# One block for turning back, gate, mix, norm and convolution; earlier turns and an early first load in the routed stages

## The reference

```
y   = gated sum of eo (expert by sequence type), s0, s1 (two shared ones)
        gate_in = concat(eo[:, 0], s0[:, 0], s1[:, 0])      # first token of each sequence
        w = softmax(relu(gate_in @ g1) @ g2)                # 3 weights a sequence
        y = eo * w[:, 0] + s0 * w[:, 1] + s1 * w[:, 2]
h   = layernorm(y); h = causal depthwise convolution of 3 taps, by channel
y   = y + attention(h)
h   = layernorm(y); e = argmax(h @ router)                  # 4 experts
y   = y + (silu(h @ Wgate[e]) * (h @ Wvalue[e])) @ Wdown[e]
out = x + y
```

## Time and profile before

| | us |
|---|---|
| median of 3 runs | 2322.33 |
| lowest, highest | 2319.68, 2323.14 |
| profiled execution, its own time | 2319.53 |
| its span, first to last instruction | 2317.7 |

### The profile page before, as it was taken

How to read it: one execution, slowest core, us unless ns; L and a number is a source line. 1 busy time by engine, 2 the same in 40 slices (tenths; PEclk the granted TensorE clock), 3 DMA queues, 4 the chain that set the end, 5 groups by cost and what they waited for, 6 DMA issues and landing times. The chain is left out here.

```text
span 2317.7 us, 32452 instructions
## 1 busy us (share of the span) xinstructions
PE 2104.6 (91%) x11748; PEld 1784.8 (77%) x11748; DVE 1213.9 (52%) x1983; ACT 906.6 (39%) x1780; POOL 763.5 (33%) x845
## 2 busy tenths in 40 slices
PE   7999999999999999999986887998996469968998
PEld 6888888888888888888875676786996158847997
DVE  3333444334443444344448993433783966657886
ACT  4232323333242323333222994122553224445554
POOL 3030302102030302103012894020783475407884
PEclk9999999999999999999997898999997688978999
DMA  4010000101010000200003003200561030036661
GB/s 156 1 55 1 36 18 0 55 0 54 0 54 0 36 18 0 79 0 0 1 2 81 25 34 119 73 10 0 182 211 62 18 82 35 34 127 220 205 200 56
DMA packets 85644, 135.73 MB, mean 59 GB/s; under 512 B 9726, under 2 KB 64000, under 8 KB 85568
## 3 DMA queue, kind: packets, MB, share of 16 engines
q1 hardware_dynamic: 78512, 118.72, 15.9%
q0 software_dynamic: 4928, 12.86, 1.6%
q10 hardware_dynamic: 2128, 3.15, 0.4%
HBM read 106.91 MB, written 12.06 MB: 51 GB/s over the span
## 5 line engine op out<-in xcount | busy, mean ns | idle before, releaser
L581 DVE TENSOR_TENSOR cond_h<-cond_silu,ps 128x512 f32<-128x512 f32 x288 | 197.9, 687 | 697.7 <-ACT cond_silu L492 694.3
L492 ACT ACTIVATE cond_silu<-ps 128x512 f32<-128x512 f32 x288 | 172.3, 598 | 772.6 <-PE ps L411 772.6
L411 PE MATMUL ps<-a_x_hi,cond_w_hi 128*128 128x512 f32 x1152 | 449.8, 390 | 2.0 <-DVE a_x_lo L261 2.0
L411 PE MATMUL ps<-a_x_lo,cond_w_hi 128*128 128x512 f32 x1152 | 449.2, 390 | 0.0
L411 PE MATMUL ps<-a_x_hi,cond_w_lo 128*128 128x512 f32 x1152 | 449.1, 390 | 0.0
L380 POOL TENSOR_TENSOR cond_w_lo<-cond_stage_up,cond_w_hi 128x256 fp32r<-128x256 f32 x144 | 108.6, 773 | 833.2 <-ACT cond_w_hi L473 833.2
L411 PEld LDWEIGHTS ps<-a_x_hi,cond_w_hi 128*128 128x128 f32 x1152 | 217.0, 188 | 47.3 <-DVE a_x_lo L261 2.4
L411 PEld LDWEIGHTS ps<-a_x_hi,cond_w_lo 128*128 128x128 f32 x1152 | 216.9, 188 | 45.2
L411 PEld LDWEIGHTS ps<-a_x_lo,cond_w_hi 128*128 128x128 f32 x1152 | 217.0, 188 | 44.9
L427 PE MATMUL ps<-cond_h_hi,cond_d_hi 128*128 128x512 f32 x576 | 224.4, 390 | 3.4 <-DVE cond_h_lo L549 3.4
L427 PE MATMUL ps<-cond_h_hi,cond_d_lo 128*128 128x512 f32 x576 | 224.1, 389 | 0.0
(11 more groups left out here) (358 smaller groups left out, 4380.8 us busy)
## 6 DMA issues: line engine op xcount, KB each, us to landing
moe_stage_up<-in_L_ffn_expert_wv SPq DMA_DIRECT2D x22, 1024.0 KB, 10.0
typed_stage_up<-in_L_cond_wi SPq DMA_DIRECT2D x11, 1024.0 KB, 4.9
typed_stage_dn<-in_L_cond_wo SPq DMA_DIRECT2D x11, 1024.0 KB
moe_stage_dn<-in_L_ffn_expert_proj SPq DMA_DIRECT2D x11, 1024.0 KB, 5.6
cond_stage_up<-in_L_cond_Wg SPq DMA_DIRECT2D x7, 1024.0 KB, 4.9
cond_stage_up<-in_L_cond_Wu SPq DMA_DIRECT2D x7, 1024.0 KB, 6.9
cond_stage_dn<-in_L_cond_Wd SPq DMA_DIRECT2D x7, 1024.0 KB, 5.2
hyp_v_now<-hyp_v_blk SPq DMA_DIRECT2D x16, 272.0 KB, 2.3
```

Of the source, the lines that this page charges most:

```text
L411: ins = pe.matmul(up_ps[st % 2][j], w[:, j, k, fs], x[:, k, tok], start=(i == 0), stop=(i == 3 * KC - 1))
L492: act.activation(silu[:, st % 2], up_ps[st % 2][0], ACT.Silu).then_inc(act_done, 1)
L581: dve.tensor_tensor(h[:, st % 2], silu[:, st % 2], up_ps[st % 2][1], ALU.mult).then_inc(up_free, 1)
```

## The change

The three blocks `turn_back`, `mix_gate` and `layer_norm` for ln1 become one, `join`:

- SP waits for the scatters inside the block, loads the first rows of the 32 sequences, [32, 256], and then the four tiles. The gate's matmuls on `s0` and `s1` start at once; those on the typed rows use the 32 turned first rows.
- The second gate weight is spread over 128 columns by ACT (`wide`), so that the logits come out on every partition, [128, 3, 32], and DVE's softmax gives the weights there.
- ACT scales the typed rows by sequence while it takes them from PSUM (8 instructions a tile). DVE adds `s0` and `s1` with 16 scalar_tensor_tensor of [128, 2, 64] a tile, each with the weight of one sequence as its scalar. POOL scales nothing.
- ACT's second affine step writes the last tap's product directly (`wt`, `bt`), so the convolution is two scalar_tensor_tensor per channel block. The inverse root stays in PSUM.
- Gate, norm, tap and attention weights are loaded by SP at the end of the typed stage (`LoadLate`), into the right side of SBUF.

In the routed stages the next rows are turned at f = 1, rounded at 2, split at 3, and ACT copies the residual half (`keep_rows`) at f = 5. In moe, expert 0 gets at least one slot (`known_first`), so slot 0 is always expert 0's, and its weights are loaded during ln2. For typed, the up weights of slot 1 are now loaded after the lists are found.

The diff, cut to its core:

```diff
+class JoinWeights:
-class GateWeights:
-def mix_gate(nc, m, gate, eo, s0, s1, w):
+def join(nc, m, eo_rows, sent, sumT, s0, s1, gate, rope):
...
+            def _(sp):
+                wait_sent(sp, sent)
+                sp.dma_start(first[:], eo_rows.rearrange("(b t) d -> b t d", t=T)[:, 0, :]).then_inc(first_loaded, 16)
+                rows = eo_rows.rearrange("(i p) d -> p i d", p=P)
+                for t in range(TT):
+                    i = slice(t * SUB, (t + 1) * SUB)
+                    sp.dma_start(y[:, i], rows[:, i]).then_inc(row_loaded[t], 16)
...
+                turn(0)
+                turn(1)
+                steps((0, means), (0, lambda t: turn(t + 2) if t + 2 < TT else None), (1, variances))
...
+                    for b in range(BT):
+                        n = t * BT + b
+                        ins = act.activation(sumT[:, :, seq(t, b)], eo_ps[t % 2][:, :, b * T:(b + 1) * T], ACT.Copy, scale=w[:, 0, n:n + 1])
...
+                        act.activation(h[:, t % 2, c, :, PAD:], x, ACT.Identity,
+                                       bias=gate.bcol[:, c:c + 1], scale=gate.wcol[:, c:c + 1]).then_inc(h_done, 1)
+                        act.activation(by_batch(convT[:, c, tile(t)]), x, ACT.Identity,
+                                       bias=bt[:, c:c + 1], scale=wt[:, c:c + 1]).then_inc(tapped, 1)
...
+                scale(0)
+                scale(1)
+                steps((2, affine), (0, lambda t: scale(t + 2) if t + 2 < TT else None), (1, inverse), (0, square))
...
+                    for j, x in ((1, s0), (2, s1)):
+                        for b in range(BT):
+                            n, at = t * BT + b, (slice(None), slice(None), seq(t, b))
+                            ins = dve.scalar_tensor_tensor(sumT[at], x[at], w[:, j, n:n + 1], sumT[at], ALU.mult, ALU.add)
...
+                mix(0)
+                mix(1)
+                steps((0, centre), (2, convolve), (0, lambda t: mix(t + 2) if t + 2 < TT else None), (1, normalize))
...
+        if self.known_first:
+            link(dve.tensor_scalar(self.used[:, 0:1], self.used[:, 0:1], 1.0, None, ALU.max))
...
     def sync(self, sp):
         sp.wait_ge(self.lists.owned, 1)
-        self.slots.load_first(sp, self.lists.found)
+        e = self.slots.expert(sp, 1)
+        self.slots.load_up(sp, e, 1)
+        sp.wait_ge(self.lists.found, 1)
+        self.slots.load_down(sp, e, 1)
...
-                        if f == 4 and not is_last(s):
+                        if f == 1 and not is_last(s):
                             turn(s + 1, nth + q, 1 - q)
...
-                            if f == 5:
+                            if f == 2:
                                 round_x(s + 1, 1 - q)
+                            if f == 5 and carried:
+                                keep_rows(s + 1, 1 - q)
...
-                    if carried:
-                        dve.tensor_copy(keep[:, q], x_row[:, q, :, D:]).then_inc(kept, 1)
...
-                        if f == 6 and not is_last(s):
+                        if f == 3 and not is_last(s):
                             split_x(s + 1, 1 - q)
...
-def turn_back(nc, m, tag, src, dst, early):
...
+                routed_ffn(nc, m, "typed", False, slots, LoadLate(joining, rope))
+            join(nc, m, m.typed_rows, sent, m.sumT, s0, s1, joining, rope)
...
+                           sync_late=lambda sp: slots.load_slot(sp, 0, 0))
```

436 lines of the change are left out of this document (233 added, 203 removed).

## The result

The changed kernel takes 2287.94 us (median of 4 runs, 2287.34 to 2288.22) against 2321.01 for the kernel before in the same comparison (2316.54 to 2323.14): a ratio of 0.9858, interval 0.9844 to 0.9871. The prediction was 2286, with 2272 to 2301 as its range. The profiled execution took 2287.70, its span is 2285.9.

What follows compares the result with a forecast made beforehand. TensorE was taken to bound the typed stage, so gains lay in the join and the last stage's start and waits. 27.1 + 6.3 + 3.0 = 36.4 us off 2319.53 gives 2283.1, plus 2.8 for the median: 2286, range 2272 to 2301.

Steps and rivals of the forecast that it cites:

- The join, behind the weights: Join from gate weights to last convolution: 47.1 us instead of 59.6, a gain of 12.5 us.
- the order of the walk: Join behind the gates: scaling, mixes, centring, normalising and convolutions followed in written order, last convolution ending at 47.1 us.
- The join, ahead of the weights: Join up to the gate weights: first rows fetched ahead of the tiles, gates at about 1779, a gain of 14.6 us.
- The rival in which they come no sooner: Join: first rows arrive no sooner than the tiles, 5 us less gain, 2291; chance 0.05.
- Typed slots, and loads behind them: Typed routed stage: the earlier turn gains 0, and the late weight loads and attention-weight splitting cost nothing.
- The last stage, its start: Start of last stage: slot 0's early expert load and sooner gathered rows bring the first turn 9.1 us earlier, net 6.3.
- The give-back: Last stage, slot 0: a VectorE cast waits for GpSimd's run, a late hidden difference gives 2.6 us back.
- The loop: Last stage's loop: waits for split rows go, half returns as lateness of hidden differences; gain 3.0 us, bounds 0 and 6.3.
- GpSimd's pace: Rival, last stage: GpSimd sets the pace, the stage gains 4 instead of 9.3 us, 2291; chance 0.2.
- The port held for one instruction: Rival, last stage: casts never wait out a GpSimd run, start keeps 9.1 us and loop 6.3, 2280; chance 0.08.
- Dear small pieces: Rival, join: steps 0.35 us apart and TensorE at 1.2 GHz, join gains 20 us, 2293; chance 0.13.
- The slower case: Rival, routed slots: the turn at step 1 waits for its gather; 2336 if landing takes 20 us; chance 0.02.

Runs made afterwards that it cites:

- e6: Changed kernel with 15 extra matmuls, results unused, behind TensorE's last matmul of the typed stage; 2284.49 us, ratio 0.9843 to the kernel before.
- e11: Changed kernel with slot 1's down weights held, three differences on VectorE, tile t+2 turned before tile t's means, 8 extra matmuls behind the typed stage; 2281.33 us.
- e3: Changed kernel with the 32 first rows loaded behind the four tiles; 2287.04 us, ratio 0.9867 to the kernel before.
- e1: Changed kernel with turn, rounding and splitting of the next rows back at steps 4, 5 and 6, kept rows still on ScalarE; 2289.31 us.
- e8: Changed kernel with only slot 1's down weights (1 MB) held until slot 0's gathered rows have landed; 2286.88 us.
- e2: Changed kernel with slot 0's expert loaded only once the owners are known, as before the change; 2291.44 us.
- e7: Changed kernel with the kept rows copied by VectorE again at step 5, the turn staying at step 1; 2289.10 us.
- e10: Changed kernel with three of slot 0's eight weight differences formed by VectorE, slot 1's loads unchanged; 2287.71 us.
- e9: Changed kernel with slot 1's down weights held until slot 0's rows have landed, and three of slot 0's eight differences on VectorE; 2284.16 us.
- e12: The e11 kernel with further extra matmuls in TensorE's waits around attention, results unused; 2278.03 us, ratio 0.9824 to the kernel before.

## Why the prediction came out right, and where its steps were off

**The join, behind the weights: right in length, its reason incomplete.** 47.57 us against 47.1. The price of the fused steps (17.4 us against 18.2), VectorE as the bound and the order of the walk held. But "the 24 larger steps removed cost 29.4" is their price beside GpSimd; alone they are about 16.6, and the gain is GpSimd's absence. By its formula for an fp32 tensor_tensor, the Trainium skill, "VectorE: DVE Perf Modes", errata of SBUF-source ops, gives about 0.29 us for one such step as an estimate; the trace has 0.346 for one and 0.27 from step to step (32 in 8.74 us).

**The join, ahead of the weights: the mechanism right, the term too large.** 9.7 us instead of 14.6 (10.3 by the clock of the trace, as the scatter was 0.6 earlier). The issue (1772.06 for 1772.0) and the landing were right. What failed is the step "Two transposes, a copy, four matmuls, two Relu and six matmuls ... about 2.6 us". I took the price of one ScalarE row for a chain of matmuls; an fp32 matmul stands as two in the rows, so four and six are 8 and 12, and each took 0.23 us at 1.2 GHz: 1.92 and 2.74. And the 16 on `s0` and `s1`, which I left out as starting at once, start with the block, at 1772.05, and end behind the landing. Rows of before had the granted clock (0.65 as a mean); I used it for the means and variances and not for the gate. e6 and e11 show the clock as part of it, e11 ScalarE's queue as the next bound.

**First rows.** The rival in which they come no sooner fell: 1.7 us from issue to landing, and e3 lost 6.1 us at the gates.

**Typed slots, and loads behind them: nearly right.** SP's loads went out from 1733.72 to 1739.35. TensorE has the same single wait in both traces (7.4 us, at the start). But where I had 0 the stage is 0.9 us shorter: 12.55 us from slot to slot instead of 12.65, a gain of the early turn that stands in no wait row (e1 has 12.65 again).

**The last stage, its start: off by its chosen value, within its bounds.** "I take 2086.0" for the landing, of bounds 2085.2 to 2089.5; in the same frame it was 2080.19 + 8.88 = 2089.07. I reckoned with 2.3 MB outstanding and an even rate; the 1 MB of slot 1's down weights, issued 0.96 us ahead of the gathers, was what they met (e8: 5.77). The gain was 6.2 where I had 9.1.

**The give-back: true, but only for the kernel I had in mind.** Forecast was a cast that waits for GpSimd's run and 2.6 us back, if the first expert matmul comes 8.5 us behind the fence. In the changed kernel it comes at 11.4, and no wait gives anything back; the 0.9 us that e2's loop is shorter go with the clock. In e8 it comes at 8.3, and 2.54 us are lost in just that wait, 4.1 with all behind it. The two errors of mine cancel: 9.1 - 2.6 - 0.2 = 6.3 forecast, 6.1 measured with the lists' 0.15.

**The loop: my gain was too small.** It is 6.7 us against 3.0. The step "the same lateness comes in every slot instead of every second. I take half" failed: the trace has no wait for a hidden row at all. Casts still fall into GpSimd's runs (one of 2.37 us at 2119.90), but with the split out of the way VectorE has the slack to take them. e7 shows that the early turn removes the waits without the copy on ScalarE. With the late turn and the copy on ScalarE, e1 has 1.0 us of waits where before had 6.3; that the copy did this is argued, not isolated.

**The rivals.** GpSimd's pace: e10 speaks against it. The port held for one instruction: against it stand the cast of 7.17 us before and that of 5.83 us in e8, over four differences in a row; the Trainium skill, "SBUF — State Buffer", "Who interferes with whom", has the lock for one instruction, and these runs don't agree with its length. That rival had the loop's gain right (6.3), for a reason that isn't shown. Dear small pieces: no, 0.27 us from step to step against that rival's 0.35. The slower case: no wait for a gather in the loop.

**What no part of the forecast had** are 3.6 us in attention and second norm, whose code is the same. I put 0 there without saying so. Against the forecast the gate misses 4.9, attention and norm 3.6, the start 2.9, the rest of the join 0.5; the loop with the give-back that didn't come has 6.3 more, and 0.6 is the earlier scatter. So 31.4 of the 36.4 us came, 5.0 less. That the time was missed by only 2 us is in part luck of another kind: I added 2.8 us because the median before lay that far above its profiled execution, and after it lies 0.2 above (2287.94, 2287.70), which takes 2.6 of the 5.0 back; 0.4 us more was gained behind the last scatter. The number owes its closeness to errors that cancel as much as to the terms.

## What to carry to other kernels

A chain of small matmuls behind an idle stretch is priced by its rows at 1.2 GHz (here 0.23 us a row of 32 columns), one by one, with all that the engine has queued ahead of it; an early landing is worth nothing before that queue is done. Where a stage's start is moved ahead, ask which engine's own work starts no sooner: the gain is kept only together with a shorter run of that engine (e8 alone brought nothing, with e9 3.2 us). A step's price in the trace holds beside its neighbours: look for the same instruction where the other engine is idle (0.69 us here, against 1.42) before saying what was saved. And where unchanged stages between can take 210 or 218 us, an edit of a few us is judged by its own stretch of the trace, not by the whole time.

## What the runs showed that I had not expected

- Stages of the same code came out at separate lengths, not spread between: attention 173.8 to 174.2 or 176.7 to 177.7 us (175.7 with its waits filled), second norm 36.3 or 40.5 to 41.4 (39.1 in e12). The lengths go with where TensorE's granted clock falls to 1.2 GHz: from 1994 to 2006 us it is 0.69 to 0.88 in after, and 1.00 in e6.
- The join starts 4.1 us behind the end of the last scatter's issue (1767.93 to 1772.01) on all engines, though only SP waits for the landing inside it. Moving that wait into the block gained nothing (before, SP's first load came 4.2 us behind that end). What holds the others there no row names.
- With 4.19 MB moved in the 20 us around the gathers, a gather took 6.1 us to land; with the 1 MB ahead of it held back, 4.1; with all of slot 1's 3 MB held, 3.4.
